# Differential attention: another place for the second head's weighted sum, the output sum in strips, and the mean square's power first

## The reference

```
q, k = rope(x @ wq.T), rope(x @ wk.T)        # 4 half-heads of 64: two for each of two heads
v    = x @ wv.T                              # 2 heads of 128
probs = softmax(q k.T / SCALING)             # 32 x 32 for each sequence and half-head
diff  = probs[head, 0] - lam * probs[head, 1]
attn  = diff @ v                             # 32 x 128 for each sequence and head
attn  = attn * rsqrt(mean(attn * attn) + 1e-5) * subln_weight   # the mean over a head's 128
x     = x + attn @ wout.T
```

## Time and profile before

| | |
|---|---|
| median of three runs | 3437.31 us |
| profiled execution, its own time | 3437.49 us |
| its span, first to last instruction | 3435.6 us |
| around the span | 1.9 us |
| TensorE busy | 3361.4 us, 98% |
| VectorE, ScalarE, GpSimd busy | 71%, 57%, 48% |
| mean granted TensorE clock | 0.994 |
| output additions of this layer (`y_d`) | 32, the first at 946.6, the last at 1106.3 us |

### The profile page before, as it was taken

How to read it: one execution, slowest core, us unless ns; L and a number is a source line. 1 busy time by engine, 2 the same in 40 slices (tenths; PEclk the granted TensorE clock), 3 DMA queues, 4 the chain that set the end, 5 groups by cost and what they waited for, 6 DMA issues and landing times.

```text
span 3435.6 us, 92591 instructions
## 1 busy us (share of the span) xinstructions
PE 3361.4 (98%) x29689; PEld 2484.9 (72%) x29698; DVE 2446.6 (71%) x7409; ACT 1960.2 (57%) x5935; POOL 1647.2 (48%) x3197
## 2 busy tenths in 40 slices
PE   9999999999899999999999999999999999999999
PEld 7888888888666767777777777777766666665555
DVE  5677877777787648888888888888868844444443
ACT  5777777777566537777776777776765411111111
POOL 4666666666565536655665565566546400000000
PEclk9999999999999999999999999999999999999999
DMA  3111111111212231111111111111135620000000
GB/s 96 57 54 53 56 53 53 55 53 56 65 51 70 81 109 44 45 46 42 44 46 42 48 46 41 45 46 42 47 79 145 184 64 20 20 19 20 19 19 9
DMA packets 280323, 187.59 MB, mean 55 GB/s; under 512 B 117165, under 2 KB 277125, under 8 KB 280213
## 3 DMA queue, kind: packets, MB, share of 16 engines
q1 hardware_dynamic: 279925, 185.75, 19.0%
q10 hardware_dynamic: 288, 0.40, 0.1%
HBM read 145.61 MB, written 36.21 MB: 53 GB/s over the span
## 4 chain that ended last, share of the span: by engine, by line
PE 51%; DVE 7%; issue 2%; ACT 2%; DMA 1%; SPq 0%; DVEq 0%; ACTq 0%; POOL 0%; POOLq 0%
PE bank_e L2551 13%; PE bank_e L2528 6%; PE a_ps_a L1011 5%; PE b_ps_a L969 5%; PE s_ps_a L976 4%; PE a_ps_a L980 3%; PE out_ps_a L1091 3%; PE c_ps_a L980 2%; PE b_ps_a L1023 2%; DVE neg_max_a L1203 2%; ACT probs_a L1112 1%; PE out_ps_a L1078 1%; PE m_ps_r L2146 1%; PE b_ps_a L1018 1%; PE b_ps_a L1036 1%
## 5 line engine op out<-in xcount | busy, mean ns | idle before, releaser
L1112 ACT ACTIVATE probs_a<-s_ps_a,neg_max_a 128x257 f32<-128x257 f32 x1024 | 472.2, 476 | 283.5 <-DVE neg_max_a L1203 283.5
L1154 POOL TENSOR_SCALAR probs_a<-probs_a,gated_a 128x256 f32<-128x256 f32 x1024 | 495.2, 503 | 269.3 <-DVE gated_a L1211 269.3
L1203 DVE TENSOR_REDUCE neg_max_a<-s_ps_a 128x1 f32<-128x257 f32 x1024 | 360.9, 414 | 0.0
L2577 ACT ACTIVATE gate_e<-bank_e 128x512 f32<-128x512 f32 x128 | 76.4, 597 | 493.1 <-PE bank_e L2551 493.0
L523 POOL TENSOR_SCALAR probs_i<-probs_i,inv_sum_i 128x256 f32<-128x256 f32 x512 | 244.8, 492 | 127.9 <-DVE inv_sum_i L687 123.4
L2694 DVE TENSOR_TENSOR hidden_e<-gate_e,bank_e 128x512 f32<-128x512 f32 x128 | 87.3, 687 | 292.5 <-PE bank_e L2551 290.9
L2509 POOL TENSOR_TENSOR inv_std_e<-var_eps_e,half_e 128x4 f32<-128x4 f32 x8 | 8.1, 1010 | 567.2 <-DVE var_eps_e L2591 567.2
L507 ACT ACTIVATE probs_i<-s_ps_i,neg_max_i 128x257 f32<-128x257 f32 x512 | 236.3, 474 | 69.7 <-DVE neg_max_i L758 68.0
L366 PE MATMUL a_ps_i<-w_k_i,ctx_t_i 128*128 128x256 f32 x1024 | 253.6, 391 | 5.5 <-issue 5.5
L1011 PE MATMUL a_ps_a<-w_v_a,ctx_t_a 128*128 128x256 f32 x1024 | 256.7, 394 | 0.0
L381 PE MATMUL c_ps_i<-w_v_i,ctx_t_i 128*128 128x256 f32 x1024 | 242.2, 379 | 0.0
(11 more groups left out here) (365 smaller groups left out, 8059.7 us busy)
## 6 DMA issues: line engine op xcount, KB each, us to landing
ctx_t_i<-in_ctx_t SPq DMA_DIRECT2D x128, 256.0 KB, 2.7
ctx_t_a<-in_ctx_t SPq DMA_DIRECT2D x128, 256.0 KB, 2.7
mask_a<-in_L_xattn_mask SPq DMA_DIRECT2D x512, 4.0 KB, 1.5
v_bd_a<-v_self_a SPq DMA_DIRECT2D x512, 8.0 KB, 1.8
x_tok_i<-in_x SPq DMA_DIRECT2D x32, 128.0 KB, 2.0
x_res_i<-in_x SPq DMA_DIRECT2D x32, 128.0 KB, 2.4
x_after<-y_tok_i SPq DMA_DIRECT2D x32, 128.0 KB, 1.7
x_tok_d<-x_after SPq DMA_DIRECT2D x32, 128.0 KB, 2.2
```

The costliest lines, as they stand in the source:

```text
L1112: act.activation(probs[:, t, :], s_ps[:, g, 0:K], ACT.Exp, bias=neg_max[:, t:t + 1], accum_out=row_sum[:, t:t + 1]).then_inc(exp_done, 1)
L1154: pool.tensor_scalar(probs[:, t, 0:2 * P], probs[:, t, 0:2 * P], gated[:, t:t + 1], 1.0, ALU.mult, ALU.mult).then_inc(probs_ready, 1)
L1203: dve.tensor_reduce(neg_max[:, 4 * f + g:4 * f + g + 1], s_ps[:, g, 0:K], AX.X, ALU.max, negate=True).then_inc(max_ready, 1)
```

## The change

The second head's weighted sum of sequence s goes to rows of sequence s+1 (mod 4), so to another column tile of the array, and into the free columns of `v_ps`' bank instead of `av_ps`. In `attn` and `attn_t` the second head's tokens are therefore shifted by one sequence, and the output sum undoes this: it is made in four strips of 32 tokens, each with the tokens of sequence s of either head. As the bank is now shared, v of chunk n+1 waits until `attn` of chunk n-2 has been read out of it, and `av` waits until v of chunk n+1 has been copied. On VectorE `ms` comes ahead of the sum `qk`; on GpSimd the power of `ms` comes ahead of that of the variance.

```diff
+    av_of = av_ps[:, 0:P], v_ps[:, D:D + P]
+
+    def place(s, c):
+
+        g = (s + c) % 4
+        return slice(L * g, L * g + L)
...
+            if live(n - 1):
+                pool.wait_ge(ms_ready, n)
+                pool.tensor_tensor(inv_rms[:, :], ms[:, :], half[:, :], ALU.pow).then_inc(rms_ready, 1)
             if live(n + 3):
                 pool.wait_ge(ln_dve, n + 4)
                 pool.tensor_tensor(inv_std[:, :], var_eps[:, :], half[:, 0:1], ALU.pow).then_inc(ln_pool, 1)
-            if live(n - 1):
-                pool.wait_ge(ms_ready, n)
-                pool.tensor_tensor(inv_rms[:, :], ms[:, :], half[:, :], ALU.pow).then_inc(rms_ready, 1)
...
             if live(n + 1):
                 ge(pe, v_ready, n + 1)
+                ge(pe, attn_ready, n - 1)
                 for c in range(2):
                     last = pe.matmul(v_ps[:, 0:D], xn_t[:, c, :], w_v[:, c, :], start=c == 0, stop=c == 1)
...
                 ge(pe, attn_ready, n - 1)
+                if live(n + 1):
+                    pe.wait_ge(v_ready, n + 2)
                 for c in range(2):
                     for s in range(4):
                         own = slice(L * s, L * s + L)
-                        last = pe.matmul(av_ps[own, c * P:c * P + P], diff_t[(n - 1) % 2][own, c * L:c * L + L], v[(n - 1) % 3][own, c * P:c * P + P], start=True, stop=True)
+                        last = pe.matmul(av_of[c][place(s, c), :], diff_t[(n - 1) % 2][own, c * L:c * L + L], v[(n - 1) % 3][own, c * P:c * P + P], start=True, stop=True)
...
                 for c in range(2):
-                    last = pe.matmul(y_ps[:, 0:D], attn_t[:, c, :], w_o[:, c, :], start=c == 0, stop=c == 1)
+                    for s in range(4):
+                        last = pe.matmul(y_ps[L * s:L * s + L, 0:D], attn_t[:, c, place(s, c)], w_o[:, c, :], start=c == 0, stop=c == 1, skip_group_check=True)
...
-                    last = act.activation(attn[:, h, :], av_ps[:, h * P:h * P + P], ACT.Copy, scale=inv_rms[:, h:h + 1])
+                    last = act.activation(attn[:, h, :], av_of[h], ACT.Copy, scale=inv_rms[:, h:h + 1])
...
-                    last = act.activation(squares[:, h, :], av_ps[:, h * P:h * P + P], ACT.Square, accum_out=ss[:, h:h + 1])
+                    last = act.activation(squares[:, h, :], av_of[h], ACT.Square, accum_out=ss[:, h:h + 1])
...
+            if live(n - 1):
+                dve.wait_ge(ss_ready, n)
+                dve.tensor_scalar(ms[:, :], ss[:, :], 1.0 / P, 1e-5, ALU.mult, ALU.add).then_inc(ms_ready, 1)
             if live(n + 1):
                 dve.wait_ge(sin_ready, n + 2)
                 dve.wait_ge(cos_ready, n + 2)
                 ge(dve, qk_t_full, n + 1)
                 dve.tensor_tensor(qk[:, :], turn_cos[:, :], turn_sin[:, :], ALU.add).then_inc(qk_ready, 1)
-            if live(n - 1):
-                dve.wait_ge(ss_ready, n)
-                dve.tensor_scalar(ms[:, :], ss[:, :], 1.0 / P, 1e-5, ALU.mult, ALU.add).then_inc(ms_ready, 1)
```

## The result

The changed kernel takes 3451.64 us (median of 7 executions, 3448.35 to 3453.21) against 3436.03 (7 executions, 3434.47 to 3438.41) before: the ratio is 1.0045, 95% interval 1.0036 to 1.0054. The profiled execution took 3452.4 us, its span is 3450.6 us, and the mean granted clock 0.993 was 0.994 before. The sign was right. The time lies outside the range, which ended at 3450.

The account below looks back on a forecast made before the run. TensorE bounds the kernel now; after the change v's wait for `attn` makes the slot 5.64 us instead of 5.38. 30 x 0.26 = +7.8, less 0.2 at the layer's end, gives +7.6: 3445.1 us, range 3435.8 to 3450.

Parts of the forecast that it names:

- Weighted sum, -0.17: TensorE's av matmuls: eight tiles with two passes each save 0.17 us per slot, bounds -0.34 and 0.
- Strips, +0.13: TensorE's y in four column strips: y and what follows it cost 0.13 us more per slot.
- TensorE's own slot, 5.34: Differential layer: without any wait TensorE's slot would be 5.34 us instead of 5.38, bounds 5.17 and 5.55.
- Step 1: Loop of v's new wait: from the scores' start to `ms` on VectorE, 2.07 us.
- Step 2: VectorE: the `qk` sum follows `ms` 0.11 us later and runs from 2.18 to 2.87.
- Step 3: GpSimd: `inv_rms` is held by the `qk` sum and ends at 3.43 us, bounds 3.02 and 3.57.
- Step 4: `attn` starts 0.04 us after `inv_rms` and ends at 4.09; TensorE starts v 0.05 later, at 4.14.
- Step 5: TensorE: v's start to the next scores takes 1.40 us plus 0.10 for v's exposed first load; slot 5.64.
- The tail, -0.2: Layer's end behind the 30 intervals: chain through av and the last y, -0.17 - 0.06 = -0.2 us.
- the case with the free return: Rival: power not held and return from strips to whole array free; slot 5.23 us, total 3433.0 us; chance 4 in 100.
- not held: Rival: `inv_rms` isn't held by the `qk` sum, v doesn't wait; slot 5.34 us, total 3436.1 us; chance 14 in 100.
- the collision of `turn_cos` and `turn_sin`: Part of the longer-loop rival: `turn_cos` may come second and collide, similar in size to 3449.3 us; longer 16 in 100.

Follow-up runs that it names:

- late_sum: Changed kernel with the `qk` sum moved behind `row_sum` and its reciprocal: 3440.35 us against 3435.9 for the kernel before, ratio 1.0012.
- strips_alone: Kernel before with only `y` in four strips of each head's own tokens, weighted sum unchanged: 3438.64 us against 3434.88, ratio 1.001.
- one_wait: Changed kernel with v's wait for the copy of v dropped where the wait for `attn` implies it: 3448.83 us against 3435.9 for the kernel before.
- old_order: Changed kernel with both swaps (`ms` and its power moved ahead) undone: 3455.32 us against 3435.9 for the kernel before, ratio 1.0058.
- after_again: The changed kernel measured once more, unaltered: 3449.96 us against 3435.73 for the kernel before, ratio 1.0042.
- rotated: Changed kernel with later `qk` sum, single wait of v, and whole-array `y`, the head shift undone in `attn`'s turn: 3434.11 us against 3434.88 before.
- code_padded: Kernel before with 24 more already-satisfied waits per slot on TensorE behind `y`: 3445.07 us against 3434.88, ratio 1.003.
- order_alone: Kernel before with nothing but the two swaps, `ms` ahead of the `qk` sum and its power first: 3437.30 us against 3435.9, ratio 1.0003.
- code_front: Kernel before with 835 further already-satisfied waits at the start of TensorE's program: 3480.30 us against 3435.73, ratio 1.0133.

## Why the prediction was wrong, step by step

The mechanism was right. Two sizes were off, and one place was left out, which weighs most: without the 5.4 us outside the differential layer the time would be 3446.2, inside the range.

- *Weighted sum, -0.17:* -0.151 measured (late_sum with strips_alone), which is -0.19 in the matmuls and +0.04 for the later start. *Strips, +0.13:* +0.137. *TensorE's own slot, 5.34:* 5.363.
- *Step 1, `ms` 2.07 after the scores:* 2.07. *Step 2, the sum 2.18 to 2.87:* 2.18 to 2.87. *Step 3, `inv_rms` held and ended at 3.43:* 3.43, with 1.114 us for 0.70; late_sum, where nothing but the sum's place changes, has 0.704. The Trainium skill's exclusion of VectorE and GpSimd ("SBUF — State Buffer", "SBUF: two separate sides") is seen, with the same 0.14 us done under the running sum that the prediction kept apart from the page's full hold. By that rule of the Trainium skill the later one is blocked whichever it is; but the sum that begins 0.35 us behind the power in late_sum takes its usual 0.69, as it did in the row of before where the power had begun 0.23 ahead. Here the measurement decides. *Step 4's first half, `attn` till 4.09:* 4.09.
- *Step 4's second half failed: TensorE 0.05 later, v at 4.14.* v starts at 4.23. The 0.05 was read in the layer's end, where the turn waits for one semaphore that comes late; v has two waits in the code, and the second costs an instruction of its own, released and then followed by the load. One_wait shows it by itself: 0.053 and a slot of 5.640.
- *Step 5, 1.50:* 1.469, the load having 0.03 head start on the matmul behind the separate wait, and 1.498 in one_wait. Steps 4 and 5 together miss 0.06 a slot; over the 30 intervals 169.70 - 160.00 = 9.7 us instead of 7.8, so 1.9 us.
- *The tail, -0.2:* +0.3 from the last scores to the layer's end. The term mis-sized is the clock: TensorE's steps there were priced at the full clock of the earlier trace rows, and in the changed kernel the half clock begins at 1106.0, with 9.7 us to go, instead of just behind the layer. Late_sum, whose half clock begins 0.3 us ahead of the end, has the forecast tail: 9.52 us where before has 9.70, -0.2. The changed kernel has 9.98. (The clock falls within 10 us of that place in every kernel, see the last section.) Another 0.2 us came in the layer's first slots.
- *The sum, "Together +7.6 us", has no term for the other five layers,* and gives no reason for that. This is the largest miss: 5.4 us of 15.6 at the median, most of it in the fifth layer, where in the profile of after TensorE is 3.6 us longer busy and 3.0 longer idle; what sets that off stays open. Nothing in the trace of before showed that this layer moves by some us with what stands ahead of it, and one profile couldn't have.

The sum again with what was measured: 30 intervals +9.7, end +0.3, start +0.2, outside the layer +5.4, together +15.6.

Two slips in the prediction's figures changed nothing: the case with the free return leaves out the -0.2 of the tail (3432.8 instead of 3433.0), and its chances add up to 0.38 for the same and 0.01 for faster.

Of the rivals, "not held" was what late_sum made of it, with the slot 0.02 longer than that rival's 5.34; the collision of `turn_cos` and `turn_sin` came, 0.6 us on VectorE in each slot, and stayed hidden; the loads of strips are hidden too. Moving `ms` and its power ahead was priced right at 0.21 us (old_order against the changed kernel).

## What to carry to other kernels

When a change gives an instruction of TensorE a second semaphore to wait for, price an instruction of its own: 0.09 us behind the event where the late one decides (0.06 of the slot here), and likely the 0.04 of av where both have long come. See first whether one of the two implies the other. When an operation is moved ahead on one engine to speed a chain up, look at what it now starts inside of on the other: the swap here gained 0.21 us although the power grew by 0.41, and moving the long sum behind two short operations gave the 0.34 back by which the slot exceeded TensorE's own. A forecast of 8 us in a kernel of 3440 should carry bounds for the layers that nobody touches, here -0.3 to +5.4 us, and one of its bounds should have the layer's end priced at half clock. Before a kernel is used as a test of code length, count its instructions in the trace: two waits were one instruction.

## What the runs showed of the hardware that was not expected

- Waits on TensorE for a semaphore that already has its value stand in the trace as one instruction for two waits, 0.106 us apart, whether 12 stand in a slot or 418 at the program's start. Behind running matmuls 1.0 of 1.3 us is hidden (+0.237 us a slot); at the start nearly nothing is (+40.3 us of 45).
- A GpSimd power that starts 0.14 into a VectorE sum takes 1.11 us for 0.70; when it starts 0.35 ahead of the sum, neither of them is longer. `turn_cos` beside a `turn_sin` that began first takes 1.30 us for 0.69 when the other began 0.10 ahead, 1.09 at 0.30 and 1.01 at 0.44: each time it ends some 1.4 us behind the other's start.
- The half clock at the differential layer's end (TensorE idles there between dependent steps) began anywhere from 9.8 us ahead of the end to just behind it (after_again 9.8 ahead, after 9.7, rotated 6.0, code_padded 6.0, order_alone 5.6, old_order 5.5, one_wait 5.4, late_sum and code_front 0.3, strips_alone at the end; before 0.1 behind). It makes y's 16 passes 1.93 us instead of 1.07.
- The fifth layer, the same code in every kernel, took 199.4 to 207.0 us.
